# A decoder of five attentions on one core: q and k planes in device memory, and row maxima as a 97th row of the contraction

## What is computed

```python
logits = jnp.einsum('bhqd,bhkd->bhqk', Q, K) * SCALE
attn = jax.nn.softmax(logits, axis=-1)
O = jnp.einsum('bhqk,bhkd->bhqd', attn, V)
```

| phase | dim of a head | keys | remarks |
|---|---|---|---|
| splat | 16 | 256 | q and k are Gaussian weights of 16 centres |
| cross0 | 16 | 120 | keys from ctx_512 |
| causal | 16 | 256 | masked before the softmax |
| self1 | 32 | 256 | masked after the softmax |
| cross1 | 32 | 120 | keys from ctx_512 |

## Time and profile before

### The profile page before, as it was taken

The page is one execution under the profiler, slowest core; times in us unless marked ns, Lnnn a source line. Parts: engine busy times, 40 slices in busy tenths (PEclk is TensorE's granted clock), DMA queues, the critical chain, the costliest instruction groups (busy, mean ns, idle before and its releaser), DMA issues. The chain is left out here.

```text
span 3813.5 us, 88266 instructions
## 1 busy us (share of the span) xinstructions
PE 3122.0 (82%) x34864; PEld 2454.4 (64%) x34864; DVE 2700.8 (71%) x6135; ACT 2106.9 (55%) x4254; POOL 978.6 (26%) x1793
## 2 busy tenths in 40 slices
PE   2988788888788878878988878798978898978886
PEld 1767566767576766656766656676756676756664
DVE  5777676778675767757767658687767677858765
ACT  4745565555456555554565545546655556456652
POOL 1312341122222321231133222212333122124310
PEclk9999898989898989989999989899989998989987
DMA  6221211112112121121122111212211112112110
GB/s 196 70 57 51 73 56 60 46 46 67 53 52 66 44 66 44 48 64 54 47 62 64 54 51 38 68 46 68 61 57 60 44 41 69 48 57 68 60 38 6
DMA packets 337676, 221.30 MB, mean 58 GB/s; under 512 B 77409, under 2 KB 309234, under 8 KB 337266
## 3 DMA queue, kind: packets, MB, share of 16 engines
q1 hardware_dynamic: 337266, 215.66, 18.9%
HBM read 122.23 MB, written 93.32 MB: 57 GB/s over the span
## 5 line engine op out<-in xcount | busy, mean ns | idle before, releaser
L1159 ACT ACTIVATE p<-bank,p_log 128x512 f32<-128x512 f32 (+2 forms) x1280 | 749.3, 585 | 1188.8 <-PE bank L851 1087.9
L1713 POOL TENSOR_TENSOR prob<-p,prob 120x256 f16<-120x256 f32 (+2 forms) x512 | 451.0, 881 | 1709.5 <-ACT prob L1160 1709.1
L1418 DVE TENSOR_REDUCE negm<-bank 128x2 f16<-128x512 f32 (+1 forms) x1280 | 675.4, 569 | 167.5 <-PE bank L814 155.1
L1160 ACT ACTIVATE prob<-bank,p_log 128x512 f16<-128x512 f32 (+2 forms) x1280 | 750.5, 586 | 0.0
L721 PE MATMUL bank<-w_exp,ident_h 128*128 128x512 f16 x1280 | 421.3, 413 | 159.2 <-DMA k_ring<-k_heads 143.6
L1348 DVE TENSOR_TENSOR prob<-p,prob 128x512 f16<-128x512 f32 (+2 forms) x768 | 487.4, 644 | 90.3 <-ACT prob L1160 85.7
L830 PE MATMUL bank<-q_ring,k_ring 80*128 80x256 f16 (+4 forms) x2048 | 446.1, 285 | 39.0 <-ACT raw L1106 14.1
L851 PE MATMUL bank<-ident_h,negm 128*128 128x256 f16 (+2 forms) x2560 | 442.1, 260 | 0.0
L1722 POOL TENSOR_SCALAR_AFFINE_SELECT probm<-prob 128x128 f16<-128x128 f16 x1024 | 327.9, 359 | 315.0 <-DVE prob L1348 315.0
L814 PE MATMUL bank<-k_ring,q_ring 80*128 80x256 f16 (+4 forms) x2560 | 370.5, 260 | 35.4 <-DVE negm L1418 34.7
L814 PEld LDWEIGHTS bank<-k_ring,q_ring 80*128 80x128 f16 (+1 forms) x2560 | 237.5, 104 | 238.3 <-issue 55.4
(11 more groups left out here) (299 smaller groups left out, 6190.3 us busy)
## 6 DMA issues: line engine op xcount, KB each, us to landing
q_ring<-q_heads SPq DMA_DIRECT2D x384, 80.0 KB, 1.9
q_heads<-q_made SPq DMA_DIRECT2D x96, 256.0 KB
k_heads<-k_made SPq DMA_DIRECT2D x96, 256.0 KB
q_ring<-q_heads SPq DMA_DIRECT2D x256, 96.0 KB, 2.0
k_ring<-k_heads SPq DMA_DIRECT2D x256, 80.0 KB, 2.1
q_heads<-q_made SPq DMA_DIRECT2D x144, 128.0 KB
k_heads<-k_made SPq DMA_DIRECT2D x144, 128.0 KB
k_ring<-k_heads SPq DMA_DIRECT2D x128, 96.0 KB, 2.2
```

Of the source, the lines that this page charges most:

```text
L1159: act(p32[0:n, g % PBUF32, 0:cols], ps[0:n, 0:cols], ACT.Exp, bias=p_log[0:n, :], scale=a.scale)
L1160: act(prob[0:n, 0, g % PBUF, 0:cols], ps[0:n, 0:cols], ACT.Exp, bias=p_log[0:n, :], scale=a.scale).then_inc(a_done, one(a_done))
L1418: v.tensor_reduce(negm[:, h * NT:(h + 1) * NT], ring_v[bank_of(e, v_full)][:, :].rearrange("p (t n) -> p t n", t=NT)[:, :, 0:ATTNS[k].keys ...
L1713: g.tensor_tensor(prob[0:n, 1, m % PBUF, 0:cols], p32[0:n, m % PBUF32, 0:cols], prob[0:n, 0, m % PBUF, 0:cols], ALU.subtract).then_inc(pp_ ...
```

## The change

The change has two parts.

**Planes in device memory.** `heads16` and `heads32` now hold each plane as one block of 128 rows, as it stands in `made`; a store writes such a block. The stack is 96 rows for both sizes of head: for dim 16, six planes, of which three hold zeros, written once in setup by 12 transfers (before: 8). A fill takes each head by itself: for a pair, two transfers for q and two for k. The rows of the stack lie in another order in the ring, the same for q and k.

**The maxima as a row.** The rings have a 97th row. In `k_ring` it holds ones (a memset in setup). In `q_ring` it holds minus the row maximum of each query: `maxima_to_row` (TensorE, between the two halves of the weighted values) waits for the maxima of heads n, n+1 and turns their four columns of `negm` by four 128-wide matmuls into a bank of `ring_a`; `row_of_maxima` (ScalarE, before turn 2) copies partition 96 of it, 512 columns, to the ring. The exact scores contract over 97 rows and need no matmuls for the maxima; a pair's first exact scores wait for the copy. The row scores contract over 96 rows, with two matmuls a head as before.

```diff
+STACKED = 96
-        self.stacked = 96 if dim == 32 else 80
 def slot_filled(m):
-    return 2 * 16 * (m // SLOTS + 1)
+    return 2 * PAIR * 16 * (m // SLOTS + 1)
...
-        q_ring, k_ring = (sb(f"{what}_ring", [96, SLOTS, PAIR, TOK], F16) for what in "qk")
-        heads16 = {what: nc.dram_tensor(f"{what}_heads16", (2, 8, 80, 2, TOK), F16).ap() for what in "qk"}
-        heads32 = {what: nc.dram_tensor(f"{what}_heads32", (2, 4, 96, 4, TOK), F16).ap() for what in "qk"}
+        q_ring, k_ring = (sb(f"{what}_ring", [STACKED + 1, SLOTS, PAIR, TOK], F16) for what in "qk")
+        heads16 = {what: nc.dram_tensor(f"{what}_heads16", (2, STACKED // 16, P, 2 * TOK), F16).ap() for what in "qk"}
+        heads32 = {what: nc.dram_tensor(f"{what}_heads32", (2, STACKED // 32, P, 4 * TOK), F16).ap() for what in "qk"}
...
+                step(g.memset(k_ring[STACKED:STACKED + 1, :, :, :], 1.0))
...
+                def maxima_to_row(pair):
+                    ps = slot("a", "row", pair[0] // PAIR)
+                    e.wait_ge(*moved("max", pair[1]))
+                    for at, g in enumerate(pair):
+                        for i in range(NT):
+                            column = ORDER[g][2] * NT + i
+                            c = (at * NT + i) * P
+                            last = mm(ps[:, c:c + P], negm[:, column:column + 1].broadcast_to([P, P]), ident_h[:, :],
+                                      start=(at, i) == (0, 0), stop=(at, i) == (PAIR - 1, NT - 1))
+                    last.then_inc(a_full, one(a_full))
+
                 def exact_scores(pair):
                     for g in pair:
...
+                        if g == pair[0]:
+                            e.wait_ge(*moved("row", g // PAIR))
                         for j, (k0, n) in enumerate(a.key_tiles):
                             i0 = j * P if a.causal else 0
-                            mm(ps[0:n, j * TOK:j * TOK + TOK - i0], kk[:, k0:k0 + n], q[:, i0:TOK],
-                               start=j == 0, stop=False)
-                        e.wait_ge(*moved("max", g))
...
-                        for i in range(NT):
...
-                            last = mm(o, negm[:, h * NT + i:h * NT + i + 1].broadcast_to([P, n]), moving,
-                                      start=False, stop=i == NT - 1)
+                            last = mm(ps[0:n, j * TOK:j * TOK + TOK - i0], kk[:, k0:k0 + n], q[:, i0:TOK],
+                                      start=j == 0, stop=not a.causal and k0 + n == a.keys)
...
                         if n >= PV_LAG:
                             weighted_values(n - PV_LAG + i)
+                        if i == 0 and n < len(ORDER):
+                            maxima_to_row((n, n + 1))
                         turn("tensor", between, n, 2 + i)
...
+                def row_of_maxima(m):
+                    e.wait_ge(a_full, upcoming(e, a_full))
+                    ps = ring_a[bank_of(e, a_full)]
+                    act(q_ring[STACKED:STACKED + 1, m % SLOTS, :, :].rearrange("o h n -> o (h n)"),
+                        ps[STACKED:STACKED + 1, :], ACT.Copy).then_inc(a_done, one(a_done))
...
                     for m in range(1, TURNS):
+                        if m == 2 and n < len(ORDER):
+                            row_of_maxima(n // PAIR)
                         turn("scalar", between, n, m)
...
-                        e.dma_start(to[:, plane * a.dim:(plane + 1) * a.dim].rearrange("c d t n -> c d (t n)"),
-                                    made[what][:, part, 0:a.tiles, :].rearrange("p t n -> p (t n)")).then_inc(stored, 16)
+                        e.dma_start(to[plane], made[what][:, part, 0:a.tiles, :].rearrange("p t n -> p (t n)")
+                                    ).then_inc(stored, 16)
...
-                    t, c = h // a.together, h % a.together
-                    for what, ring, cols in (("q", q_ring, TOK), ("k", k_ring, a.keys)):
-                        e.dma_start(ring[0:a.stacked, m % SLOTS, :, 0:cols],
-                                    heads_dram(what, k, b)[c:c + PAIR, :, t, 0:cols].rearrange("c r n -> r c n")
-                                    ).then_inc(ring_full[m % SLOTS], 16)
+                    for at in range(PAIR):
+                        t, c = (h + at) // a.together, (h + at) % a.together
+                        for what, ring, cols in (("q", q_ring, TOK), ("k", k_ring, a.keys)):
+                            e.dma_start(ring[0:STACKED, m % SLOTS, at, 0:cols],
+                                        heads_dram(what, k, b)[:, c * a.dim:(c + 1) * a.dim, t * TOK:t * TOK + cols]
+                                        .rearrange("l d n -> d l n")).then_inc(ring_full[m % SLOTS], 16)
```

More of the change, by code:

```diff
@@ L497, in _ @@
                     for buffer in range(2):
[L498 to L501, removed]
+                        for plane in (3, 4, 5):
+                            e.dma_start(heads16[what][buffer, plane].rearrange("(p a) n -> p (a n)", a=4),
+                                        hidT[0:32, :, :, :].rearrange("p a t n -> p (a t n)")).then_inc(zeros_stored, 16)
                 for b in range(LANES):
@@ L510, in _ @@
                 e.wait_ge(w_ready[1], w_count[1])
-                e.wait_ge(zeros_stored, 16 * 8)
+                e.wait_ge(zeros_stored, 16 * 12)
             @block.gpsimd
@@ L794, in values, with operands @@
                             token_major(ws, col, 512, src, n_in, [tile], "a", *what, by="dve")
-                def operands(g):
+                def operands(g, rows):
                     a, h = ATTNS[ORDER[g][0]], ORDER[g][2]
                     slot_of, at = g // PAIR % SLOTS, h % PAIR
-                    return q_ring[0:a.stacked, slot_of, at, :], k_ring[0:a.stacked, slot_of, at, 0:a.keys]
+                    return q_ring[0:rows, slot_of, at, :], k_ring[0:rows, slot_of, at, 0:a.keys]
                 def row_scores(pair):
@@ L807, in row_scores @@
                             e.wait_ge(ring_full[g // PAIR % SLOTS], slot_filled(g // PAIR))
-                        q, kk = operands(g)
+                        q, kk = operands(g, STACKED)
                         ps = slot("v", "max", g)
@@ L822, in exact_scores @@
                 def exact_scores(pair):
                     for g in pair:
-                        a, h = ATTNS[ORDER[g][0]], ORDER[g][2]
-                        q, kk = operands(g)
+                        a = ATTNS[ORDER[g][0]]
+                        q, kk = operands(g, STACKED + 1)
                         ps = slot("a", "p", g)
+                        if g == pair[0]:
+                            e.wait_ge(*moved("row", g // PAIR))
                         for j, (k0, n) in enumerate(a.key_tiles):
@@ L829, in exact_scores @@
                             i0 = j * P if a.causal else 0
-                            mm(ps[0:n, j * TOK:j * TOK + TOK - i0], kk[:, k0:k0 + n], q[:, i0:TOK],
-                               start=j == 0, stop=False)
-                        e.wait_ge(*moved("max", g))
-                        n = a.key_tiles[0][1]
-                        rows = ps[0:n, :].rearrange("p (j c) -> p j c", j=NT)
-                        if a.causal:
[L836 to L839, removed]
@@ L853, in exact_scores @@
+                        if a.causal:
+                            blocks = ps[:, :].rearrange("p (j c) -> p j c", j=NT)[:, :, 0:P]
+                            last = mm(blocks, ident_h[:, :], mask_k[:, :].rearrange("p (a n) -> p a n", a=1
+                                                                                    ).broadcast_to([P, NT, P]),
+                                      start=False, stop=True)
                         last.then_inc(a_full, one(a_full))
```

## The result

| | before | after |
|---|---|---|
| median | 3819.5 us | 4283.7 us (4277.3 to 4288.3, 4 runs) |
| ratio | | 1.121, 95% interval 1.119 to 1.123 |
| span of the profiled execution | 3813.5 us | 4281.2 us |
| mean granted clock | 0.915 | 0.882 |

The changed kernel is 464 us slower. The forecast was 3925 us, slower by 105, with a range that ended at 4090: the direction was right, the loss was more than four times the forecast one.

The account below looks back on a forecast made before the run. TensorE was taken to bound the kernel, closely fed by VectorE and ScalarE. Columns -43, DMA parts -65, zero stores +2 and new waits +213 made +107 on 3820: 3927, said as 3925 us; range 3715 to 4090.

Parts of the forecast that it names:

- I take 213: TensorE's new waits for maxima and copy: net loss 213 us, the low end of 213 to 456.
- Minus 43 us for the columns: TensorE's matmuls that add the maxima: 163,840 columns go, 75 us at the mean clock, of which 14/24 counted.
- Forecast minus 63 us with the zero stores: Planes in device memory: DMA parts together minus 65 us, four more zero stores in setup plus 2 us.
- 20 us for fills: Four fill issues per pair on SP for two: 0.9 us more at each of 24 ring waits, plus 20 us.
- 85 with the clock: Stores as planes: TensorE's ring waits lose 51 us and 25 us; fewer stretches at half clock, minus 9 us.
- a gross 608 us: Delay of TensorE by late maxima and copy, before idle time absorbs any: 22.8 us in 24 pairs, 608 in 640.
- the 42 pieces of the earlier trace: VectorE sat idle before a maxima instruction in only 42 pieces for 640 pairs, so the maxima come late.
- the forecast's own signs: Maxima and copy waits: under 100 us favours no needed run-ahead; above 450, others unchanged, rival B; others shrinking, absorption undersized.
- rival B: All new waits of TensorE are real, 456 us, with the bank taken from the turns: 4170 us, chance 0.10.
- It also takes one of three banks: ScalarE's copy and the turned maxima use a bank of the ring shared with the turns; no separate size given.
- A ring wait less was credited with 9 us: Shorter ring stalls of TensorE leave fewer stretches at half clock: minus 9 us.
- The copy: ScalarE's 640 copies of one 512-column row: 581 ns each, 372 us more, total hidden beside TensorE.

Follow-up runs that it names:

- e1: The kernel before with only the planes in device memory (96-row stacks, four fills a pair), maxima as before: 3749.7 us, ratio 0.983.
- e9: The planes alone plus, for each pair, one 8-column matmul in a bank of the exact scores' ring and one 8-column copy by ScalarE: 3903.9 us, ratio 1.022.
- e8: As e6, but ScalarE copies 8 columns and not 512: 3889.6 us, ratio 1.019.
- e6: The changed kernel without TensorE's waits for VectorE's maxima and for ScalarE's copy, nothing subtracted: 3924.0 us, ratio 1.027.
- e11: The planes alone, laid out in device memory so that a pair needs two fills and not four: 3705.0 us, ratio 0.970.
- e10: The planes alone, with each 256-wide matmul that adds the maxima cut to 128 columns: 3747.3 us, ratio 0.982.
- e12: As e9, but the bank comes from the ring of the row scores, with semaphores of its own: 3816.9 us, ratio 0.9995.
- e7: The changed kernel with two more idle 512-wide matmuls per pair ahead of the wait for VectorE's maxima: 4196.8 us, ratio 1.099.

## Why the prediction was wrong

Two terms of the sum failed. "I take 213" for the new waits was too small: they cost 360 us. And the third user of the ring of banks stood at nothing, where one costs 154 us together with its two small instructions. Minus 43 us for the columns was wrong too, but smaller. Each step from the planes alone to the changed kernel is now a run, or the difference of two; another order of the steps would share the total out differently:

| step | us | from |
|---|---|---|
| planes alone | 3750 | e1 |
| a third user in the ring of banks, two tiny instructions | +154 | e9 |
| turned columns for subtracted ones | -14 | e8 - e9 |
| a copy of 512 columns, not 8 | +34 | e6 - e8 |
| the two waits | +360 | after - e6 |
| changed kernel | 4284 | |

**Planes, fills: the total right by two errors.** Forecast minus 63 us with the zero stores, measured minus 67. The stores last as long as forecast (3 us; SP waits 3.2 at most): SP's waits for k planes fell from 240.9 to 24.7 us, the longest ring wait from 14.8 to 8.3. The share of 0.70 is more than eight of 16 engines, as the number-of-engines rule of the Trainium skill ("DMA: Bandwidth & Descriptors", "Why a DMA increments its semaphore by 16 and not by 1") had it. But the fills were priced at the issue time of the old ones, 0.31 to 0.45 us; with one head each they take 0.60, so a pair holds SP for 2.4 us. e11, with two fills at the old issue time, gives 45 us back, and its ring wait is 43 us shorter; the forecast had 20 us for fills. So the stores brought more than forecast, about 113 us for 85 with the clock, and the fills took more back: that the total fits is luck. e11 also changes the layout that the stores write, so the 45 us are of fills and layout together. That it is the short pairs in which the issue time is no longer hidden was not tested.

**Columns: failed.** Minus 43 us was forecast (75 at full), e10 shows zero; in the changed kernel the exchange of columns brings 14 us (e8 - e9). Spacing by columns was read rightly (the four turning matmuls of a pair take 0.22 us in the kernel after, from 2191.42 to 2191.64), but TensorE's own time is not what sets the length where the columns went: it met the other engines sooner, and the rest came back as a lower clock. The case itself gave a hint, as VectorE sat idle before the maxima only 42 times; that this is the reason is argued, not shown.

**The new waits: right mechanism, wrong size.** Both waits are where they were forecast, the stand of the long pair (6 us for 5.52) and the loop of the short pair as well. The failed step is "I take 213": 35% of a gross 608 us, on the ground that every idle microsecond of TensorE absorbs delay and that VectorE's lateness is partly backlog. Measured are 360 us (372 in the profiled executions). The gross was not far off, 517 us of new waits for 608. Idle time did absorb, but less than assumed: TensorE's other idle time is 246 us shorter than in e6, about half of 517, where the forecast let 395 of 608 go. So 270 us of standing are left, 52% and not 35%, and 102 us of slower work, for which the term had nothing, come on top. Nor did the stands clear VectorE's lateness. Its main wait before the maxima, to hold against the 42 pieces of the earlier trace rows:

```profile
DVE negm L1427 <- PE bank L814: 101.5, 78, 7.8
```

In most of the 640 pairs it still has something else to do when the row scores arrive. Which idle time absorbs was not tested; a likely reading is that a wait for a result that hangs on the engine's own earlier work moves with the delay: TensorE's wait for the normalised z rows still stands at 76.4 us, for 100.8 before. By the forecast's own signs the case lies between the forecast and rival B: the new waits exceed 450 us, but the other waits shrink.

**The bank: named, not priced.** "It also takes one of three banks" had no term. With its two small instructions it costs 154 us, of which at least 87 hang on the ring that gives the bank (e12). The rival B, 4170 us, had it in words only and was given one chance in ten.

**The clock: left out on the way up.** A ring wait less was credited with 9 us; for new stands nothing was charged. 362 us more at half level; e7 takes 482 of the 1010 us away and wins 87 us net of all that its own columns cost outside the waits. TensorE's busy time, forecast 50 to 80 us lower, is 140 higher.

The copy was right: it takes 589 ns, for 581 forecast, and its length is mostly hidden where no wait hangs on it (34 us of 262, e6 and e8). ScalarE is busy for 58% of the longer span, where near 65% was forecast.

## What to carry to other kernels

When a value that was awaited an iteration later is awaited in the same one, price the wait with its gross lateness, take off idle time with care (here about half of the new waits was absorbed), and add the slower work behind each stand: here 270 us of standing brought 102 us more of it. Count the users of every ring of buffers per iteration: a new one with hardly any work of its own can cost more than the work. Columns saved on an engine that two others feed can be no time saved, as here; and a transfer's number of issues, each with its own price on the queue, is a term beside its bytes.

## What was not expected of the hardware

- More work, less time: 1280 idle 512-wide matmuls put in front of the wait for the maxima made the kernel 2% faster (4284 to 4197 us), the granted clock going from 0.882 to 0.937.
- Less work, no less time: 163,840 columns fewer left 3747 for 3750 us and a granted clock of 0.920 for 0.925.
- A fill that moves half the bytes is dearer to issue: a median of 0.60 us on SP with rows that stride over planes (e1), 0.31 to 0.45 us for two heads as one run of rows.
